# Attention with two kinds of weights: the values weighed on sixteen 32x32 tiles of TensorE instead of four 64x64 ones, with new PSUM buffers and a new order of the engines

## What is computed

```python
# 8 heads of 16 channels; xn is the normalised input of one sequence
q, k = rope(xn @ Wq.T), rope(xn @ Wk.T)
v = xn @ Wv.T
attn = softmax(where(causal, q @ k.T / 4, -inf))            # first kind of weights
out = attn @ v
qp = einsum('bhtd,hd->bht', q[..., :3], head_dirs)
kp = einsum('bhtd,hd->bht', k[..., :3], head_dirs)
geo_attn = softmax(where(causal, qp[:, :, :, None] * kp[:, :, None, :], -inf))   # second kind
geo_out = geo_attn @ v
out = out + head_scales * (geo_out - out)
return x + heads_joined(out) @ Wo.T
```

## Time and profile before

| | |
|---|---|
| time, median of three runs | 2090.66 us |
| span of the profiled execution, first to last instruction | 2032.5 us |
| attention phase in it | about 87 to 534.5 us |
| rounds of the attention | 32 |

### The profile page before, as it was taken

The page is one execution under the profiler, slowest core; times in us unless marked ns, Lnnn a source line. Parts: engine busy times, 40 slices in busy tenths (PEclk is TensorE's granted clock), DMA queues, the critical chain, the costliest instruction groups (busy, mean ns, idle before and its releaser), DMA issues. The chain is left out here.

```text
span 2032.5 us, 50931 instructions
## 1 busy us (share of the span) xinstructions
PE 1619.2 (80%) x17727; PEld 1257.5 (62%) x17727; DVE 1466.2 (72%) x4083; ACT 1193.9 (59%) x2778; POOL 1095.1 (54%) x1141
## 2 busy tenths in 40 slices
PE   5599999999689679398956777777789616999994
PEld 4477777777577534244424555555578616999993
DVE  8677778787379734389978999999668623555555
ACT  5555556556259932187846888888456504655551
POOL 3277777787100058423345888888726773444440
PEclk8799999999799979699978999999877657999998
DMA  3000000000321123422000000000221112222216
GB/s 121 14 3 4 3 4 3 3 3 3 143 88 40 40 35 47 108 79 63 21 0 1 1 1 1 1 1 2 92 107 48 51 60 61 65 65 65 65 50 253
DMA packets 84954, 92.34 MB, mean 45 GB/s; under 512 B 11696, under 2 KB 69296, under 8 KB 84000
## 3 DMA queue, kind: packets, MB, share of 16 engines
q1 hardware_dynamic: 67840, 62.66, 9.7%
q0 software_dynamic: 14560, 22.24, 4.2%
q10 hardware_dynamic: 2304, 4.20, 0.5%
HBM read 46.14 MB, written 42.91 MB: 44 GB/s over the span
## 5 line engine op out<-in xcount | busy, mean ns | idle before, releaser
L2275 POOL TENSOR_TENSOR delta_A<-delta_A,delta_sW 128x256 f32<-128x256 f32 x256 | 193.5, 756 | 78.7 <-ACT delta_sW L2122 52.6
L2045 PE MATMUL delta_u<-delta_m,tables_sb 128*128 128x256 f32 x512 | 166.3, 407 | 82.0 <-DVE delta_m L2195 82.0
L694 ACT ACTIVATE attn_p_att<-attn_score,attn_mx 128x32 f32<-128x32 f32 (+7 forms) x512 | 149.8, 407 | 131.2 <-DVE attn_mx L756 131.0
L2895 POOL DMA_INDIRECT choice_rows<-ffn_y,ffn_xg x135 | 129.4, 959 | 171.1 <-DVE ffn_y L3002 167.7
L2122 ACT ACTIVATE delta_sW<-delta_W,tables_sb 128x256 f32<-128x256 f32 x256 | 126.7, 505 | 79.3 <-DVE delta_W L2217 75.5
L2045 PEld LDWEIGHTS delta_u<-delta_m,tables_sb 128*128 128x128 f32 x512 | 87.0, 190 | 132.6 <-DVE delta_m L2195 125.9
L2041 PE MATMUL delta_u<-delta_v_own,tables_sb 128*128 128x256 f32 x512 | 153.7, 383 | 9.6 <-DVE xnT L2182 9.6
L2852 POOL DMA_INDIRECT rows<-mix_rows,mix_slot x128 | 124.7, 974 | 49.4 <-issue 40.4
L1324 POOL DMA_INDIRECT exp_rows<-rows,slot_token x32 | 33.0, 1030 | 197.2 <-SPq L142 187.8
L756 DVE TENSOR_REDUCE attn_mx<-attn_score 128x4 f32<-128x1024 f32 (+3 forms) x128 | 98.5, 807 | 55.9 <-PE attn_score L614 54.2
L2217 DVE TENSOR_TENSOR delta_W<-delta_W,delta_u 128x128 f32<-128x128 f32 x512 | 133.6, 282 | 4.5
(11 more groups left out here) (396 smaller groups left out, 4691.9 us busy)
## 6 DMA issues: line engine op xcount, KB each, us to landing
ffn_xg<-rows SPq DMA_DIRECT2D x135, 66.0 KB, 1.9
acc<-route_zero SPq DMA_DIRECT2D x10, 832.0 KB
comb_rows<-choice_rows SPq DMA_DIRECT2D x32, 256.0 KB, 5.4
rows<-route_rows SPq DMA_DIRECT2D x8, 640.0 KB, 3.5
load_rows<-in_x SPq DMA_DIRECT2D x16, 256.0 KB, 4.1
bT<-acc SPq DMA_DIRECT2D x16, 256.0 KB, 4.0
qT<-acc SPq DMA_DIRECT2D x16, 256.0 KB, 4.8
x_kept<-xT SPq DMA_DIRECT2D x16, 256.0 KB, 2.1
```

Of the source, the lines that this page charges most:

```text
L694: last = nc.scalar.activation(p_att[:, gr, PAIR_OFF[n]:PAIR_OFF[n] + SLOT * (n + 1)], S[:, gr, c:c + SLOT * (n + 1)], ACT.Exp, bias=mx[:, ...
L2045: nc.tensor.matmul(corrections(h, pp % 2), g.t("same_head"), m1[:, h].rearrange("p t d b -> p (t d b)"), start=False, stop=True).then_inc( ...
L2275: nc.gpsimd.tensor_tensor(A[:, t % 8], A[:, (t - 1) % 8], sW[:, t % RING], ALU.add).then_inc(k.A, 1)
L2895: nc.gpsimd.indirect_dma_start(g.choice_rows, bass.IndirectOffsetOnAxis(xg[:, n % RING, D:D + 1].bitcast(U32), 0), y[:, n % RING, :], None ...
```

## The change

- **Weighing.** One `weigh(b, par)` replaces `weigh_att` and `weigh_geo`. The stationary operand is `v_one`: for each head its 16 channels and the column of ones, 32 columns, without zeros for another head. 8 blocks, 4 heads, 2 kinds, 2 groups make 128 calls on sixteen 32x32 tiles: the head gives the row of tiles, kind and group the column. It waits for seven semaphores.
- **PSUM.** One tensor `shared` of four banks replaces `q_rows_ps`, `k_wide_ps` and `out`. The left half of each bank is the result of a head; the right halves hold projections, values, the two lines and the output of `mix`. TensorE has therefore new waits, so that it writes no bank half that is still to be read.
- **Joining the kinds.** `head_scales` is multiplied into `Wo` once at the start (two small VectorE instructions), `mix` adds the kinds in two accumulating matmuls, and GpSimd's `combine` is one instruction instead of three. `turn_mixed` turns 128x512 instead of 128x256.
- **Values.** VectorE transposes them straight into `v_one`; `spread_values` with its two GpSimd instructions goes.
- **Order.** `front_qk` of round b+2 is written between `scores` 0 and 1, `mix` runs two rounds behind, `turn_out` stands at the head of VectorE's round, `rotate` runs a round earlier on GpSimd, `gate` a round later on ScalarE.

The core of the diff:

```diff
-        v_rows = s.sb("v_rows", [128, KB, GROUPS, DH0])
-        v_diag = s.sb("v_diag", [128, GROUPS, KB, 2, SLOT])
+        v_one = s.sb("v_one", [128, 2, KB, GROUPS, SLOT])
...
-        q_rows_ps, k_wide_ps = (s.ps(name) for name in ("q_rows", "k_wide"))
-        O = s.ps("out", (128, PAIRS, 2 * T))
+        shared = s.ps("shared", (128, PER, 2 * T))
+        O = shared[:, :, 0:T]
+        raw, value = shared[:, 0:2, T:2 * T], shared[:, 0, T:2 * T]
+        q_line, k_line, mixed = shared[:, 2, T:2 * T], shared[:, 3, T:2 * T], shared[:, 2, T:2 * T]
...
-            def weigh(kind):
+            def weigh(b, par):
+                pe.wait_ge(k.straight, min(b + 3, B))
+                pe.wait_ge(k.v_turned, min(b + 2, B))
+                pe.wait_ge(k.keys_copied, min(b + 2, B))
+                if b > 1:
+                    pe.wait_ge(k.gated, b - 1)
+                pe.wait_ge(k.out_turned, b)
+                pe.wait_ge(by_unit[B_].exped, b + 1)
+                pe.wait_ge(k.att_turned, len(TURNS) * (b + 1))
                 for n in range(KB):
-                    for pair in range(PAIRS):
-                        rows = slice(HALF * pair, HALF * pair + HALF)
-                        for gr in both:
...
-                            last = nc.tensor.matmul(O[HALF * gr:HALF * gr + HALF, pair, kind * T + SLOT * n:kind * T + T],
-                                                    v_diag[rows, gr, n], weights,
-                                                    start=n == 0, stop=n == KB - 1, tile_position=(HALF * pair, HALF * gr))
+                    for h in range(PER):
+                        rows = slice(SLOT * h, SLOT * h + SLOT)
+                        for kind in range(2):
+                            for gr in both:
...
+                                col = SLOT * (GROUPS * kind + gr)
+                                last = nc.tensor.matmul(O[col:col + SLOT, h, SLOT * n:T], v_one[rows, par, n, gr, :], weights,
+                                                        start=n == 0, stop=n == KB - 1, skip_group_check=True,
+                                                        tile_position=(SLOT * h, col))
+                last.then_inc(k.weighed, 1)
...
             def mix(b):
-                pe.wait_ge(k.v_turned, min(b + 2, B))
+                if b == 0:
+                    pe.wait_ge(k.wo_ready, PAIRS)
+                pe.wait_ge(k.moving, min(b + 4, B))
+                pe.wait_ge(k.gated, b)
                 pe.wait_ge(k.mixed_turned, b + 1)
-                nc.tensor.matmul(k_wide_ps[:, T:2 * T], wo[:, :], ao[:, :], start=True, stop=True).then_inc(k.out_made, 1)
+                for side in range(PAIRS):
+                    last = nc.tensor.matmul(mixed, wo[:, side, :], ao[:, :, side, :], start=side == 0, stop=side == PAIRS - 1)
+                last.then_inc(k.out_made, 1)
...
             def front_qk(b):
-                pe.wait_ge(k.keys_copied, b)
-                pe.wait_ge(k.moving, b)
+                pe.wait_ge(k.v_turned, b)
...
-                pe.wait_ge(k.straight, b + 1)
+                else:
+                    pe.wait_ge(k.out_turned, b - 1)
+                pe.wait_ge(k.keys_copied, b)
...
                 if more:
+                    front_geo(b + 1, 1 - par)
                     front_v(b + 1)
-                    front_geo(b + 1, 1 - par)
...
```

More of the change, by code:

```diff
@@ L646, in _ @@
+                last.then_inc(k.out_made, 1)
             front_qk(0)
             pe.wait_ge(k.cleared, 3)
-            pe.wait_ge(k.ones, PER)
+            pe.wait_ge(k.ones, 1)
             front_geo(0, 0)
@@ L651, in _ @@
             scores(0, 0, 0)
+            front_qk(1)
             scores(0, 0, 1)
[L653 removed]
             for b in range(B):
@@ L660, in _ @@
                 if more:
+                    front_geo(b + 1, 1 - par)
                     front_v(b + 1)
-                    front_geo(b + 1, 1 - par)
                 geo(b, par, B_, GEO_B)
+                if b > 1:
+                    mix(b - 2)
                 if more:
                     scores(b + 1, 1 - par, 0)
-                    scores(b + 1, 1 - par, 1)
-                weigh_att(b)
-                if b > 0:
-                    mix(b - 1)
                 if b + 2 < B:
                     front_qk(b + 2)
-                weigh_geo(b)
+                if more:
+                    scores(b + 1, 1 - par, 1)
+                weigh(b, par)
+            pe.wait_ge(k.out_turned, B)
+            mix(B - 2)
             mix(B - 1)
@@ L790, in _ @@
             dve.wait_ge(k.cleared, 3)
-            for h in range(PER):
-                nc.vector.memset(v_diag[SLOT * h:SLOT * h + SLOT, :, :, h % 2, DH0:DH0 + 1], 1.0).then_inc(k.ones, 1)
+            nc.vector.memset(v_one[:, :, :, :, DH0:DH0 + 1], 1.0).then_inc(k.ones, 1)
             dve.wait_ge(k.w_in, 64)
-            nc.vector.tensor_copy(share[:, :, 1], hs[:, :]).then_inc(k.share_ready, 1)
-            nc.vector.tensor_scalar(share[:, :, 0], hs[:, :], -1.0, 1.0, ALU.mult, ALU.add).then_inc(k.share_ready, 1)
+            nc.vector.tensor_scalar(share[0:HALF, :], hs[0:HALF, :], -1.0, 1.0, ALU.mult, ALU.add).then_inc(k.share_ready, 1)
+            nc.vector.tensor_copy(share[HALF:128, :], hs[HALF:128, :]).then_inc(k.share_ready, 1)
+            dve.wait_ge(k.share_ready, 2)
+            for side in range(PAIRS):
+                nc.vector.tensor_scalar(wo[:, side, :], wo[:, side, :], share[:, side:side + 1], None, ALU.mult).then_inc(k.wo_ready, 1)
             for kind in range(2):
@@ L866, in rotate @@
                 nc.gpsimd.tensor_tensor(qk[:, par], straight[:, :, :], crossed[:, :, :], ALU.add).then_inc(k.qk_ready, 1)
-            def spread_values(b):
-                pool.wait_ge(k.v_turned, b + 1)
-                pool.wait_ge(k.geo_weighed, b)
-                for gr in both:
-                    diagonal(v_diag[:, gr, :, :, 0:DH0], v_rows[:, :, gr, :], g.t("own_in_pair"), 2, DH0).then_inc(k.v_diag, 1)
             def spread_queries(b, par):
@@ L896, in _ @@
             spread_keys(0, 0)
-            pool.wait_ge(k.share_ready, 2)
-            pool.wait_ge(k.ones, PER)
+            rotate(1, 1)
             for b in range(B):
@@ L901, in _ @@
                 more = b + 1 < B
-                if b > 1:
-                    add(b - 2)
-                if more:
-                    rotate(b + 1, 1 - par)
-                spread_values(b)
                 if more:
@@ L912, in _ @@
                     spread_keys(b + 1, 1 - par)
+                if b > 1:
+                    add(b - 2)
+                if b + 2 < B:
+                    rotate(b + 2, par)
+            combine(B - 1)
             add(B - 2)
-            combine(B - 1)
             add(B - 1)
@@ L3133, in launch_arrays @@
     out["dirs"] = dirs.reshape(128, 2, 128)
-    out["hs"] = np.repeat(a["L0_attn_head_scales"][to_head].reshape(2 * GROUPS, 1, PAIRS), SLOT, 1).reshape(D, PAIRS)
+    out["hs"] = np.tile(np.repeat(a["L0_attn_head_scales"].reshape(GROUPS, PAIRS, 2).swapaxes(1, 2).reshape(2 * GROUPS, PAIRS), DH0, 0), (2, 1))
     out["gate_w"] = a["L0_ffn_gate_w"].T
```

148 lines of the change are left out of this document (61 added, 87 removed).

## The result

The changed kernel takes 2193.69 us (median of 4 runs, 2191.25 to 2196.91) against 2088.31 us for the kernel before (4 runs, 2084.63 to 2097.49): ratio 1.0508, 95% interval 1.0481 to 1.0535. It is 105 us slower, where 2075 us was predicted, within 2061 to 2108. The sign and the range both missed.

What follows compares the result with a forecast made beforehand. It took a ring of two halves, 6.77 us on TensorE and 6.44 on VectorE, to bound the kernel. Savings of 13.0 us over 31 rounds and 2.3 at the ends took 15.3 off 2090.7: 2075 us, range 2061 to 2108.

Steps and rivals of the forecast that it cites:

- What bounds the kernel: Attention round: a closed chain of waits, 6.77 us on TensorE and 6.44 on VectorE with hand-over; neither engine alone.
- the ring after: Attention round in the new order: seven steps one after the other, 12.79 us against 13.21, saving 0.42 us a round.
- Step 1: Start of the new round on TensorE: weighing 2.55 us instead of 4.45, plus 0.15 until `turn_out` starts, 2.70 together.
- calls decide: Rival for the weighing: TensorE takes 28 ns a call whatever the tiles, 3.6 us; time 2109, slower; chance 0.19.
- Clock: Sign in the attention rounds: the forecast would be wrong if the granted clock fell below 1.00.
- The 58.2 us "around the span": Whole program: difference between median 2090.66 and profiled span 2032.5 us, taken to lie around the span and kept unchanged.
- Ends: Outside the 31 intervals: one more weighing saves 1.90 us, the steps after the last weighing 0.4; together 2.3.
- A rule of overhead: Weighing calls: about 25 ns a matmul, by estimate 3.2 us for 128 calls; held contradicted by records 7 ns apart.

## Why the prediction was wrong, point by point

- **What bounds the kernel, and the ring after: right.** The order of releases, and all of the ring but the weighing, came as worked out where no gap disturbs it: 10.09 us predicted, 10.10 in the run with half the blocks, 4.59 against 4.67 for `mix` to weighing in the changed kernel itself.
- **Step 1, the weighing of 2.55 us: wrong, 3.63 us without its gaps, 1.08 too little a round.** It took 32 starts of records 7 ns apart as the price of a narrow block (0.22 us) and left the weight loads out; a call is two loads and two matmuls. The widest block took 0.46 us, as foretold, but those of 128, 96, 64 and 32 columns took 0.47, 0.42, 0.36 and 0.34 us, 1.60 together instead of 0.88, and the rest of the 1.08 lies in the wide ones. The row of whole calls, 28 ns each, was there and gives 3.6; it was made the upper bound and argued down. On its own this slip, 31 x 1.08 us, turns the forecast of 2075 into 2109, the rival "calls decide". That rival had the sign and this term right, and its chance of 0.19 was too low; but its 2109 is still 85 us short, and its mechanism, 28 ns a call whatever the tiles, is not what the runs show (17 ns for narrow calls on sixteen tiles, 27 on four, 33 for the wide ones). That the mean is 28.4 is in part luck.
- **A term that was not in the sum: the supply of instructions.** This is the larger failure, for the sum held nothing for it. The prediction counted the calls and never asked how they reach the engine. The gaps inside the weighing are 43.8/31 = 1.41 us a round. Outside it, `turn_out` to `mix` takes 0.92 us more than predicted. Gaps behind a landing (1.0 to 1.7 us), counted over the whole stretch, are 89.3 us in the changed kernel, 45.5 of them outside the weighing, and 12.5 us in the one before, where by the count they are ordinary waits that fell beside one. Sum: 12.79 + 1.08 + 1.41 + 0.92 = 16.20 us of 16.34. How the 0.92 divides between gaps outside the weighing and the lower clock was not measured apart.
- **The demand could have been worked out in advance.** The records of a round rise from 619 to 879, which the change itself tells; the transfers of 16 KB come every 5.6 us before (73 in 408.2 us) and every 4.8 us after (106 in 506.7), but in the weighing one is wanted every 1.8 us. The supply, one in about 3.6 us, could not be read from the rows of before, where no weighing stands still behind a landing.
- **Clock: the warning was given, its cause not seen.** The text named a fall below 1.00 as a sign of failure. It fell to 0.94, as the consequence of idle gaps, which the run with doubled calls shows in one weighing and the clock records of the changed kernel in 13 places.
- **The 58.2 us "around the span": misread.** In the changed kernel span and time of the same execution differ by 2.1 us (2189.2 and 2191.35). Outside the first and last transpose the profiled execution of before took 2032.5 - 408.2 = 1624.3 us and the changed kernel 2189.2 - 506.7 = 1682.5, the very 58.2: that execution of before was presumably on another chip than the timed ones, since in later sets the kernel before takes 2037 us on one and 2086 on another. It did no harm, since only differences were summed.
- **Ends:** 98 of the 105.4 us of loss are in the rounds. The ends were to give 2.3 us and cost about 5: the first transpose starts at 123.4 us instead of 119.5, and the last addition to x ends 7.7 us after the last transpose's start (637.07 + 0.72) instead of 6.7; some 2 us are not attributed. In the last round VectorE's rows are these. `turn_out` has waited for the weighing as before; from its start to `turn_mixed`'s it is 3.49 us, in which the two steps that GpSimd lost are gone, but `turn_mixed` now waits for the `mix` of the round before it:

```profile
630.09 1.25 DVE L777 STREAM_TRANSPOSE attn_oT<-attn_shared 128x1024 f32<-128x1024 f32 x1 [5.52 <-PE attn_shared L631]
...
633.58 0.71 DVE L787 STREAM_TRANSPOSE attn_ao<-attn_scaled 128x512 f32<-128x512 f32 x1 [1.85 <-PE attn_shared L643]
```

- **A rule of overhead.** The rows first: 28.4 ns a call in the changed kernel. The prediction set the rule of the Trainium skill, "TensorEngine Tiling (Array Packing)", section "Instruction Overhead" (about 60 cycles a matmul, 25 ns at 2.4 GHz), against the 7 ns between records, and sided with the latter. The mean fp32 call of the changed kernel came near the rule; for 16-bit calls (8.7 ns) and narrow fp32 ones (17 ns) on sixteen tiles it is too high, so the nearness tells little.

- **A rule of fetching**, which the prediction did not use. The rows first: 33 gaps and 43.8 us inside the weighings, each 1.19 to 1.60 us behind a 16 KB transfer. The Trainium skill, "Runtime: NRT & Kernel Launch", section "Instruction fetch mechanics", describes such refills in blocks of 256 instructions and calls the cost of crossing a block mostly hidden. The size of the block agrees (252 loads and matmuls a packet). That it is hidden holds for the kernel before, and not for a burst of 512 records in 3.63 us.

## What to carry to other kernels

Before a change that makes matmuls more and smaller, write down the number of instruction records per round (four for an fp32 call here, two for a 16-bit one) and how fast each burst wants them, and compare it with how often a 16 KB block of instructions can arrive (about 3.6 us here); when the burst is faster, making its work cheaper only makes its gaps longer. Price a dense burst by the densest whole calls of the trace, weight loads included and on as many tiles if there are such, not by the distance of two starts. And when a term leaves the bound engine, ask which order leaves the other engines free: here the kernel before with 16-bit calls and two steps moved came to 0.963 of its set, the changed one with 16-bit calls to 0.984 of its own, though they differ in more than the order.

## What the runs showed of the hardware

- TensorE's instructions come in blocks of 16 KB; where a dense weighing stands still, it goes on 1.2 to 1.6 us after a block has landed (140 gaps in the weighings of four kernels, medians 1.39 to 1.43 us); the next transfer starts 1.10 us or a little more after the engine has gone on.
- The granted clock went from 1.00 to 0.50 during a stand of 2.6 us inside a dense weighing, and was still there when work was back.
- The same call on sixteen 32x32 tiles costs 8.7 ns in 16 bits, 17 ns in fp32 with 32 columns where nothing pauses (both some 4.2 to 4.3 ns a record), 28.4 ns in fp32 on average over 256 to 32 columns, and 33 ns over the four widest blocks. On four 64x64 tiles a narrow fp32 call costs 27 ns. Why the narrower blocks of the changed kernel take 22 to 30 ns a call and not 17 stays open; their sum does not depend on the order of the blocks.
